# A sorted tree layer on one core: the first turn of every tile written out, sums and stores behind its first half, bias products in bank 1, register loads in groups of four

## The reference

```
for _ in range(DEPTH + 1):                       # 8 levels
    all_nodes.append(current)
    score = einsum('td,td->t', flat_x, w1s[current]) + b1s[current]
    all_logits.append(score)
    choice = ((sign(score) + 1.0) / 2.0).astype(int32)
    current = current * 2 + choice + 1
path_weights = gelu(abs(logits), approximate=False)
for i in range(DEPTH + 1):
    t_i = einsum('td,tdo->to', flat_x, w2s[nodes_i]) + b2s[nodes_i]
    out = out + t_i * path_weights[:, i][:, None]
```

## Time and profile before

| | us |
|---|---|
| median of three runs | 131.72 |
| the profiled execution's own time | 130.12 |
| its span, first to last instruction | 128.4 |
| first product of the turns begins | 82.73 |
| last addition of VectorE begins (L1229) | 124.64 |
| busy: TensorE, VectorE, ScalarE, GpSimd | 106.4, 93.6, 68.8, 38.1 |

### The profile page before, as it was taken

One profiled execution on the slowest core, in us unless ns is written; L12 is line 12 of the kernel. 1 busy time (PEld: TensorE's weight loads), 2 busy tenths in 40 slices (PEclk: granted clock), 3 DMA queues, 4 the chain that ended last, 5 costly groups with the idle time before them and its releaser, 6 DMA issues.

```text
span 128.4 us, 3400 instructions
## 1 busy us (share of the span) xinstructions
PE 106.4 (83%) x980; PEld 77.2 (60%) x981; DVE 93.6 (73%) x296; ACT 68.8 (54%) x160; POOL 38.1 (30%) x67
## 2 busy tenths in 40 slices
PE   6899799649999999998899569989898988997910
PEld 2259464317656656575748236488687977977900
DVE  2789799989688979982588898655466475757480
ACT  4047368645696797792119388356433535543510
POOL 6393000000000000000040000355479659885623
PEclk9999999995999999999999999999999999999995
DMA  3996799998998000002989000030002002020000
GB/s 82 329 314 198 332 490 419 393 482 378 439 475 347 36 3 0 5 0 80 372 367 455 20 0 0 0 84 2 23 3 28 0 0 20 0 23 0 0 0 20
DMA packets 3662, 19.97 MB, mean 156 GB/s; under 512 B 417, under 2 KB 2336, under 8 KB 3136
## 3 DMA queue, kind: packets, MB, share of 16 engines
q1 hardware_dynamic: 2576, 18.68, 36.1%
q0 software_dynamic: 496, 0.33, 2.1%
q10 hardware_dynamic: 576, 0.79, 2.0%
HBM read 19.27 MB, written 0.52 MB: 154 GB/s over the span
## 4 chain that ended last, share of the span: by engine, by line
PE 39%; DVE 17%; issue 8%; DVEq 8%; ACT 6%; POOL 1%
PE turn_ps L751 10%; PE s_ps L907 6%; DVE early L1213 6%; DVEq L92 5%; PE s_ps L697 4%; PE turn_ps L907 2%; ACT prob L528 2%; PE misc_ps L716 2%; PE aux_ps L716 2%; PE turn_ps L926 2%; DVE token_path L1119 2%; DVEq L97 2%; PE s_ps L784 1%; PE s_ps L636 1%; ACT prob_t L524 1%
## 5 line engine op out<-in xcount | busy, mean ns | idle before, releaser
L528 ACT ACTIVATE prob<-prob,negmax 128x512 f32<-128x512 f32 x32 | 21.7, 716 | 5.5 <-DVE negmax L1079 5.5
L1079 DVE CUSTOM_DVE_ANT_0 prob<-s_ps,mask 128x512 f32<-128x512 f32 x32 | 21.0, 686 | 3.3 <-PE s_ps L697 2.6
L751 PE MATMUL turn_ps<-ident,prob 128*128 128x128 f32 x128 | 20.1, 294 | 3.4 <-ACT prob L528 3.4
L437 POOL TENSOR_TENSOR early<-early,scaled_sb 128x256 f32<-128x256 f32 x24 | 19.1, 796 | 11.5 <-ACT scaled_sb L608 9.6
L1213 DVE SCALAR_TENSOR_TENSOR early<-s_ps,coef,early 128x128 f32<-128x128 f32 x40 | 12.2, 347 | 13.5 <-issue 6.3
L907 PE MATMUL s_ps<-w,msg 128*128 x128 | 18.5, 287 | 2.9 <-issue 1.6
L751 PEld LDWEIGHTS turn_ps<-ident,prob 128*128 128x128 f32 x128 | 14.6, 147 | 10.2 <-ACT prob L528 8.9
L907 PEld LDWEIGHTS s_ps<-w,msg 128*128 128x128 f32 x128 | 15.5, 191 | 5.8 <-issue 5.7
L403 POOL TENSOR_TENSOR rstd<-veps,mhalf 128x2 f32<-128x2 f32 x2 | 1.4, 714 | 54.0 <-DVE veps L950 54.0
L608 ACT ACTIVATE scaled_sb<-s_ps,coef 128x128 f32<-128x128 f32 x24 | 8.8, 368 | 11.2 <-PE s_ps L907 11.1
L907 PE MATMUL turn_ps<-w,msg 128*128 x64 | 9.8, 275 | 0.0
(11 more groups left out here) (204 smaller groups left out, 201.8 us busy)
## 6 DMA issues: line engine op xcount, KB each, us to landing
w<-in_w_t SPq DMA_DIRECT2D x3, 4096.0 KB, 22.9
w<-in_w_t SPq DMA_DIRECT2D x1, 4032.0 KB, 13.5
w<-in_adj SPq DMA_DIRECT2D x1, 1024.0 KB, 9.0
w_sb<-in_w_t ACTq DMA_DIRECT2D x1, 384.0 KB, 4.7
x_sb<-in_x SPq DMA_DIRECT2D x1, 256.0 KB, 3.0
msg<-in_neigh_t SPq DMA_DIRECT2D x1, 256.0 KB, 4.5
out_x<-x SPq DMA_DIRECT2D x1, 256.0 KB, 3.8
row_sb<-in_rows ACTq DMA_DIRECT2D x1, 255.5 KB, 7.4
```

What stands on the lines that cost most here:

```text
L437: nc.gpsimd.tensor_tensor(mine, mine, scaled_sb[:, slots[0]:slots[-1] + 1, :], ALU.add).then_inc(pooled[i], TURN)
L528: nc.scalar.activation(prob[:, u % RING, :], prob[:, u % RING, :], ACT.Exp, bias=negmax[:, t, h:h + 1], scale=-1.0).then_inc(exped, 1)
L751: last = nc.tensor.transpose(turn_ps[u % 2][:, m * P:(m + 1) * P], prob[:, u % RING, m * P:(m + 1) * P], ident[:])
L1079: nc.vector.tensor_tensor_reduce(out=prob[:, u % RING, :], in0=score_ps[u % RING], in1=mask[:, t, :], scale=1.0, scalar=0.5 * MASKED, op0= ...
```

## The change

Five edits.

1. `tile_turns`: for every tile the first turn is now written out, and the loop runs from the second turn to the end. The loop has at least one pass: every tile's length is turned up to at least 32 entries (`turned_up`, `list_lengths`).
2. `after` of a tile is called ahead of the next tile's first turn by TensorE and ScalarE, and behind that turn's first half by VectorE and GpSimd (`late=True`). With it go two waits: GpSimd waits for `bias_moved` ahead of its first addition of tiles 1 and 2, VectorE for `read_back` at the start of tile 3's first turn.
3. `BIAS_BANK` is 1 instead of 4. The wait for `bias_moved` stands in the written turn alone, at bank 1.
4. Register loads of VectorE and ScalarE are of 4 or 8 entries: VectorE's second half reads 8 instead of 6, ScalarE's second half 4 instead of 2.
5. Tile 3's last sums: GpSimd's two are added to two of VectorE's at once, those two together, and the sum that is ready last at the end.

```
-BIAS_BANK = 4
+GROUP = 4
+BIAS_BANK = 1

-        entries[0:1, 0:TILES], engines=(engine,), min_val=TURN, max_val=NODES_PAD,
+        entries[0:1, 0:TILES], engines=(engine,), min_val=2 * TURN, max_val=NODES_PAD,

-def tile_turns(eng, lengths, turn, begun, after):
-
-    def whole_turn(s, e, at):
+def tile_turns(eng, lengths, turn, begun, after, late=False):
+
+    start = end = STEP
+    for s in range(TILES):
+        if s > 0 and not late:
+            after(s - 1, end)
         for half in range(HALVES):
-            turn(s, half, e + half * STEP, at + half * STEP)
-
-    start = STEP
-    whole_turn(0, STEP, 0)
-    begun()
-    for s in range(TILES):
+            turn(s, half, start + half * STEP, s * NODES_PAD + half * STEP)
+            if s > 0 and late and half == 0:
+                after(s - 1, end)
+        if s == 0:
+            begun()
         end = eng.snap((lengths[s] & (2 * NODES_PAD - TURN)) + start)
-        with eng.Fori(start + TURN if s == 0 else start, end, TURN) as e:
-            whole_turn(s, e, e - start + s * NODES_PAD)
-        after(s, end)
+        with eng.Fori(start + TURN, end, TURN) as e:
+            for half in range(HALVES):
+                turn(s, half, e + half * STEP, e - start + s * NODES_PAD + half * STEP)
         start = end
+    after(TILES - 1, end)
...
             def add_scaled(s, half, e, at):
+                if isinstance(at, int) and half == 0 and 1 <= s <= len(BIASED_AFTER):
+                    pool.wait_ge(bias_moved, s)
...
-                    if s == 0:
-                        pool.wait_ge(read_back, 16)
...
-                own_entries(nc, nc.scalar, entry[0:len(ACT_BANKS[half])], nodes, at, len(DVE_BANKS[half]))
+                own_entries(nc, nc.scalar, entry[0:GROUP], nodes, at, GROUP)
...
-                    if half == 0 and j == BIAS_BANK and 1 <= s <= len(BIASED_AFTER):
+                    if half == 0 and j == BIAS_BANK and 1 <= s <= len(BIASED_AFTER) and isinstance(at, int):
                         pe.wait_ge(bias_moved, s)
...
-            nc.vector.tensor_scalar(turned_up[:, 0:1], length[:, 0:1], TURN - 1.0, 2.0 * TURN, ALU.add, ALU.max)
-            then(nc.vector.tensor_scalar(turned_up[:, 1:TILES], length[:, 1:TILES], TURN - 1.0, float(TURN),
-                                         ALU.add, ALU.max))
+            then(nc.vector.tensor_scalar(turned_up[:], length, TURN - 1.0, 2.0 * TURN, ALU.add, ALU.max))
...
-                own_entries(nc, nc.vector, entry[0:len(DVE_BANKS[half])], nodes, at, 0)
+                own_entries(nc, nc.vector, entry[0:-(-len(DVE_BANKS[half]) // GROUP) * GROUP], nodes, at, 0)
...
+                if isinstance(at, int) and half == 0 and s == READ_BACK:
+                    dve.wait_ge(read_back, 16)
...
             def sum_up(s, end):
-                for _, j in DVE_ORDER[-DVE_SUMS:]:
-                    dve.wait_ge(emptied[j], end)
-                nc.vector.tensor_reduce(dve_sum[:, s, :], acc[:, 0:DVE_SUMS, s, :].rearrange("p j d -> p d j"),
-                                        AX_X, ALU.add).then_inc(halved, 1)
                 if s < TILES - 1:
-                    if s + 1 == READ_BACK:
-                        dve.wait_ge(read_back, 16)
+                    for _, j in DVE_ORDER[-DVE_SUMS:]:
+                        dve.wait_ge(emptied[j], end)
+                    nc.vector.tensor_reduce(dve_sum[:, s, :], acc[:, 0:DVE_SUMS, s, :].rearrange("p j d -> p d j"),
+                                            AX_X, ALU.add).then_inc(halved, 1)
                 else:
+                    for _, j in DVE_ORDER[-DVE_SUMS:-1]:
+                        dve.wait_ge(emptied[j], end)
                     dve.wait_ge(pooled[-1], end + STEP)
-                    dve.wait_ge(halved, TILES)
-                    then(nc.vector.tensor_tensor(dve_sum[:, s, :], dve_sum[:, s, :], acc[:, DVE_SUMS, s, :], ALU.add))
-                    nc.vector.tensor_tensor(result[:, s, :], dve_sum[:, s, :], acc[:, DVE_SUMS + 1, s, :], ALU.add
+                    mine = acc[:, 1:DVE_SUMS, s, :]
+                    then(nc.vector.tensor_tensor(mine, mine, acc[:, DVE_SUMS:SUMS, s, :], ALU.add))
+                    then(nc.vector.tensor_tensor(dve_sum[:, s, :], acc[:, 1, s, :], acc[:, 2, s, :], ALU.add))
+                    dve.wait_ge(emptied[DVE_ORDER[-1][1]], end)
+                    nc.vector.tensor_tensor(result[:, s, :], dve_sum[:, s, :], acc[:, 0, s, :], ALU.add
                                             ).then_inc(tile_done, 1)
```

More of the change, by code:

```diff
@@ L113, in list_lengths @@
     _, lengths = nc.values_load_multi_w_load_instructions(
-        entries[0:1, 0:TILES], engines=(engine,), min_val=TURN, max_val=NODES_PAD,
-        skip_runtime_bounds_check_because="lengths are counts of nodes turned up to at least one turn")
-    return lengths
-def tile_turns(eng, lengths, turn, begun, after):
-    def whole_turn(s, e, at):
-        for half in range(HALVES):
-            turn(s, half, e + half * STEP, at + half * STEP)
-    start = STEP
-    whole_turn(0, STEP, 0)
-    begun()
-    for s in range(TILES):
+        entries[0:1, 0:TILES], engines=(engine,), min_val=2 * TURN, max_val=NODES_PAD,
+        skip_runtime_bounds_check_because="lengths are counts of nodes turned up to at least two turns")
+    return lengths
+def tile_turns(eng, lengths, turn, begun, after, late=False):
[3 more added lines that the diff above has]
+            after(s - 1, end)
+        for half in range(HALVES):
+            turn(s, half, start + half * STEP, s * NODES_PAD + half * STEP)
[3 more added lines that the diff above has]
+            begun()
         end = eng.snap((lengths[s] & (2 * NODES_PAD - TURN)) + start)
-        with eng.Fori(start + TURN if s == 0 else start, end, TURN) as e:
-            whole_turn(s, e, e - start + s * NODES_PAD)
-        after(s, end)
+        with eng.Fori(start + TURN, end, TURN) as e:
+            for half in range(HALVES):
+                turn(s, half, e + half * STEP, e - start + s * NODES_PAD + half * STEP)
         start = end
+    after(TILES - 1, end)
 def gnn_ffn_kernel(nc, x, adj, neigh_t, w_t, cols, rows, w1_t, w2_t, b2, out):
@@ L465, in store @@
                         ap=token_s[:, s:s + 1], axis=0), in_=result[:, s, :], in_offset=None).then_inc(stored, 16)
-            tile_turns(nc.gpsimd, lengths, add_scaled, read_last, store)
+            tile_turns(nc.gpsimd, lengths, add_scaled, read_last, store, late=True)
             pool.wait_ge(stored, 16 * TILES)
@@ L608, in scale @@
                     nc.scalar.activation(scaled_sb[:, slot, :], product_ps[j], ACT.Copy,
-                                         scale=coef[:, s, bass.ds(node_at(nc.scalar, entry, i), 1)]
+                                         scale=coef[:, s, bass.ds(node_at(nc.scalar, entry, len(DVE_BANKS[half]) - GROUP + i), 1)]
                                          ).then_inc(emptied[j], STEP)
@@ L1217, in sum_up @@
             def sum_up(s, end):
-                for _, j in DVE_ORDER[-DVE_SUMS:]:
-                    dve.wait_ge(emptied[j], end)
-                nc.vector.tensor_reduce(dve_sum[:, s, :], acc[:, 0:DVE_SUMS, s, :].rearrange("p j d -> p d j"),
-                                        AX_X, ALU.add).then_inc(halved, 1)
                 if s < TILES - 1:
-                    if s + 1 == READ_BACK:
-                        dve.wait_ge(read_back, 16)
-                else:
+                    for _, j in DVE_ORDER[-DVE_SUMS:]:
+                        dve.wait_ge(emptied[j], end)
+                    nc.vector.tensor_reduce(dve_sum[:, s, :], acc[:, 0:DVE_SUMS, s, :].rearrange("p j d -> p d j"),
+                                            AX_X, ALU.add).then_inc(halved, 1)
+                else:
+                    for _, j in DVE_ORDER[-DVE_SUMS:-1]:
+                        dve.wait_ge(emptied[j], end)
                     dve.wait_ge(pooled[-1], end + STEP)
-                    dve.wait_ge(halved, TILES)
-                    then(nc.vector.tensor_tensor(dve_sum[:, s, :], dve_sum[:, s, :], acc[:, DVE_SUMS, s, :], ALU.add))
-                    nc.vector.tensor_tensor(result[:, s, :], dve_sum[:, s, :], acc[:, DVE_SUMS + 1, s, :], ALU.add
+                    mine = acc[:, 1:DVE_SUMS, s, :]
[3 more added lines that the diff above has]
+                    nc.vector.tensor_tensor(result[:, s, :], dve_sum[:, s, :], acc[:, 0, s, :], ALU.add
                                             ).then_inc(tile_done, 1)
-            tile_turns(nc.vector, lengths, add_up, lambda: None, sum_up)
+            tile_turns(nc.vector, lengths, add_up, lambda: None, sum_up, late=True)
 _INS = ("x", "adj", "neigh_t", "w_t", "cols", "rows", "w1_t", "w2_t", "b2")
```

## The result

The changed kernel is slower by 1.8%: ratio of its runs to those of the kernel before 1.0184, 95% interval 1.0149 to 1.022. The lowest times of the two are 2.3 us apart.

What follows compares the result with a forecast made beforehand. The turns were taken to be bound by a ring of engines, VectorE's sequencer rather than its engine, TensorE nearly as long. Terms: 4.4 - 0.8 - 0.6 - 0.3 - 0.2 + 0.1 = +2.6 us, giving 134.3 us, range 131.9 to 136.0.

Steps and rivals of the forecast that it cites:

- One turn more: Tile 2 takes two turns instead of one, 9 in all; a plain turn more, +4.4 us, bounds 4.1 and 4.8.
- Loads: VectorE's second-half load of 8 saves 0.15 us, counted in 5 or so of 9 turns: -0.8, bounds -1.4 and -0.3.
- Rival C: Register load costs 136 ns per register, so eight make 1.09 us, in eight turns or so: 137.7 us; chance 0.03.
- Jumps back: Loop jumps back fall from 3 to 1, in tile 3 alone: -0.2 us, bounds -0.6 and 0.
- GpSimd: Sums and store between GpSimd's two halves delay later additions, but the delay ends just in time: 0, bounds 0 and +1.5.
- Rival B: GpSimd's store in the middle holds up ScalarE, so banks 1 and 6; three joins lose about 1 us each: 137; chance 0.09.
- Joins after tiles 0 and 1: Bias products wait for bank 1, emptied early by ScalarE, instead of bank 4: -0.6 us for both, bounds -1.4 and +0.3.
- Join after tile 2: VectorE's step to the next tile, without sum and jump, gets shorter; TensorE allows part: -0.3 us, bounds -0.5 and 0.
- The end: Tile 3's last sums: nothing gained, GpSimd rather than VectorE's shorter load sets the end: +0.1 us, bounds -0.2 and +0.3.
- Rival A: Joins and loads of six were the dear thing; 3.9 us saved against 4.4, so not slower, 132.2 us; chance 0.24.
- Rival D: The ninth turn doesn't appear or is free: 129.9 us; chance 0.04.

Runs made afterwards that it cites:

- experiment 8: Changed kernel keeping only the written turns (9 turns), with old loads, bias bank, sums' place and last sums: ratio 1.0242 to the kernel before, turns 45.14 us.
- experiments 1: Kernel before with every tile's length at least 32 entries, so 9 turns, nothing else changed: ratio 1.0343 to the kernel before, turns 46.66 us.
- experiment 6: Changed kernel with GpSimd's sums and store moved behind the next tile's whole written turn: ratio 1.0114 to the kernel before, turns 43.61 us.
- experiment 5: Changed kernel with the bias products in bank 4 again: ratio 1.0152 to the kernel before, turns 44.02 us.
- experiment 7: Changed kernel with VectorE's sums and GpSimd's sums and store ahead of the next tile again: ratio 1.0161 to the kernel before, turns 43.26 us.
- experiment 3: Kernel before with only the register loads changed, VectorE's 8 instead of 6, ScalarE's 4 instead of 2: ratio 0.9989 to the kernel before, turns 41.37 us.
- experiment 4: Changed kernel with the old register loads of six and two entries: ratio 1.0202 to the kernel before, turns 45.11 us.
- experiment 12: Changed kernel with conditions around the loops (8 turns), sums and stores ahead of the next tile: ratio 0.977 to the kernel before, turns 39.23 us.

## Why the prediction was right, and which of its steps were not

It said 2.6 us more, 2.0%; the turns became 2.36 us longer, the ratio is 1.8%. On the scale of the three runs it gave 134.3 us; the 20 runs have 132.58, inside the range of 131.9 to 136.0 but low in it; the medians themselves moved by only 1.08 us. The size of the sum is partly luck. Along the path of experiment 8 the extra turn came as forecast (4.5 for 4.4), the written turns gave 1.5 where the sum has 0.2, bank, loads and last sums gave 1.9 where it has 1.3, and the late sums and store cost 1.3 where it has a gain of 0.3: two gains came out larger than forecast and a third turned out a loss, and the errors cancel.

- **One turn more, +4.4: right.** 4.3 to 4.5 us in the old order, 4.2 in the new. The counts of 64, 64, 32, 96 and the length rule decided the sign.
- **Loads, -0.8: near in size.** 0.8 in the old order, 0.55 in the new, which is the one that the term is about; the load itself became 0.61 us, shorter than the 0.66 taken, and less of it came through. Rival C, by the register, falls: eight take less than six. By the rule of 200 ns per register in the Trainium skill, "Runtime: NRT & Kernel Launch", section "Instruction fetch mechanics", it would be 1.6 us by estimate (the page speaks of registers loaded from HBM, these lists lie in SBUF); the measured 0.607 decides.
- **Jumps back, -0.2, and "I count no gain from fewer address sums": wrong.** The written turns with their three jumps fewer gave 1.5 us (experiments 1 and 8). The bounds there, -0.6 and 0, were too narrow, even with the 0.3 for the third jump that the price of the extra turn contains (4.4, against 4.1 without its jump). I had read one gap of 0.30 at a jump back of VectorE. That the jumps and address sums of the other engines in the ring count too is a likely reason, but no run tries them one by one.
- **GpSimd, 0, bounds 0 and +1.5: wrong value, right bounds.** It cost 0.95 us. The step said the delay "ends just about there", some 2 us into the next turn. In experiment 6, with no delay, ScalarE reached bank 1 at 3.0 us into that turn; with the store in the middle it could only at 4.3, 1.3 us too late, and by the same reckoning 0.1 and 0.4 too late in the next two tiles. Tile 0 has a third sum (L460), 0.5 us of it; the rest of the difference was not taken apart. Rival B was this mechanism: ScalarE waited for GpSimd at all three joins, but only at one did more than 0.14 us reach TensorE.
- **Joins after tiles 0 and 1, -0.6: right at the first, wrong at the second.** 0.4 was forecast and 0.4 came (experiment 5). At the second the step took ScalarE to empty bank 1 early; held up by the store it did not, and 0.8 was lost against bank 4. The wait at bank 1 came as worked out: 1.8 us from the bias products' start to bank 1 (93.79 to 95.57), where the step had 1.7.
- **Join after tile 2, -0.3: wrong.** VectorE's step got 0.25 shorter, TensorE's turn not at all (experiment 7). The sum was hidden ahead as well as behind.
- **The end, +0.1: somewhat wrong.** The last turn is 6.26 us against 6.46 with new loads and old sums (experiment 3's kernel), and with old loads 6.33 (experiment 4's) against 6.55 (experiment 8's): a gain of about 0.2, though other things differ in both pairs. GpSimd does set the end, as said: the 128x256 addition waits 0.30 for it and takes 0.42.

Rival A didn't happen: the change gave back 2.1 of the extra turn's 4.4 us, not 3.9. But it was nearer than that says: with the sums and the store ahead of the tile (experiment 7) 3.4 come back, 1.5 of them by the written turns and 1.9 by bank, loads and last sums. Rival D falls with the counts.

## What to carry to other kernels

Where a loop is cut open so that its first pass is written out, ask first what its least number of passes becomes, and count passes per case in the trace: here that one row was worth more than all the rest, and a condition around the loop kept the gain at a cost of about 0.1 us, by the estimate above. Work that is moved off one engine's path into the middle of a ring should be followed through the engines behind it: a store that nobody waits for delayed an addition, that a scaling, and that a matmul a whole turn later. And what one sequencer saves pays only as far as the next engine's own sequence allows: of 0.21 us a load, nine times, 0.55 us came through.

## What the runs showed of the hardware

A register load of two entries takes longer than one of four, and one of six longer than one of eight: 487 and 308 to 317 ns on ScalarE, 816 and 607 on VectorE. Over all turns but the first, two take 487 to 503 ns and four 306 to 321 on ScalarE, six 811 to 831 and eight 595 to 645 on VectorE. The first load of the second half, in tile 0's first turn, is longer in each case: 784 and 588 ns on ScalarE, 1001 and 770 on VectorE.

An addition of GpSimd that follows its indirect store is recorded with 1.26 to 1.31 us instead of 0.72 in the changed kernel, at all three joins. Its record begins while that of the DMA's issue still runs, and it ends 0.75 to 0.77 us behind the issue's end (103.29 behind 100.89 + 1.64), so the rows don't show a slower addition: the engine is taken up by the issue for 1.54 to 1.64 us, and the addition comes after it.

The first product comes at 81.53 to 84.47 us in kernels whose code ahead of it is all but the same, and the granted clock of TensorE up to 82 us mostly goes with it: at 1.00 it comes between 81.53 and 82.64, at 0.98 between 82.53 and 82.73, at 0.96 between 83.30 and 84.27, and at 0.94 at 84.47. The page's row of it (40 slices, tenths of full speed) for experiment 7's kernel, first product at 84.47, and for experiment 12's, at 81.53:

```profile
PEclk9999999856999999999958999999999999999995
```

```profile
PEclk9999999999999999999999999999999999999996
```

In the first the clock is at its lower level (1.2 GHz, half) for all of slice 9, most of 10 and 21 and part of 8 and 22, in the second nowhere before the last slice. In the turns it is at full speed in both. Two profiles of one kernel say the same: those of the changed kernel are 1.6 us apart in time and 1.67 in the first product, those of the kernel before 0.8 and 0.89. In these pairs the difference between runs is made ahead of the stage that was changed, and there a single stage's length in one profile tells small steps apart that six runs cannot. What makes the clock fall in one execution and not in the next I did not find out.
